# Expert-choice FFN in units of two batches, with half of the add-backs moved into the next attention

## The reference

```python
def _L0_ffn_ref(x, gate_w, w1, w2):            # x: 8 x 512 x 128, E = 8 experts
    probs = softmax(einsum('ntd,ed->nte', x, gate_w))
    g, m = top_k(probs.transpose(0, 2, 1), k)  # k = 128 tokens of each batch for each expert
    xin = x[batch_idx, m]
    h = gelu(einsum('nekd,edf->nekf', xin, w1))          # 128 -> 512
    h = einsum('nekf,efd->nekd', h, w2)                  # 512 -> 128
    return zeros.at[batch_idx, m].add(g[..., None] * h)
...
x = x + ga * _L0_attn_ref(h, ...)
x = x + gb * _L0_ffn_ref(h, ...)               # the rows added back are needed, batch by batch,
x = x + ga * _L1_attn_ref(h, ...)              # before that batch's layer-1 attention
```

## Time and profile before

| | us |
|---|---|
| runs | 1907.9, 1910.45, 1912.4 |
| median | 1910.45 |
| profiled execution | 1909.73 |
| its span | 1907.4 |
| attention 0 and what lies ahead of it | 0 to 814.7 |
| expert-choice FFN | 814.7 to 1013.9 |
| transfers | to 1042.62 |
| attention 1, then the top-2 FFN and the output | to 1907.4 |

### The profile page before, as it was taken

The page is one execution under the profiler, slowest core; times in us unless marked ns, Lnnn a source line. Parts: engine busy times, 40 slices in busy tenths (PEclk is TensorE's granted clock), DMA queues, the critical chain, the costliest instruction groups (busy, mean ns, idle before and its releaser), DMA issues.

```text
span 1907.4 us, 75393 instructions
## 1 busy us (share of the span) xinstructions
PE 1648.4 (86%) x34316; PEld 1268.5 (67%) x34316; DVE 1054.0 (55%) x2219; ACT 695.3 (36%) x1071; POOL 880.8 (46%) x836
## 2 busy tenths in 40 slices
PE   6899999999999988888563889989999998878993
PEld 4567777777777666665342667767777777767883
DVE  3656666666697854536110556665666666544324
ACT  2334444344344323343220333433333433334341
POOL 2555555565646476337886303334242342015442
PEclk9999999999999989999786999999999998989997
DMA  9700000000000000053326223132321313026666
GB/s 305 248 6 2 8 2 7 2 8 2 8 2 8 2 22 20 19 126 35 61 35 117 57 51 81 46 83 51 75 73 44 88 42 84 20 66 183 204 209 183
DMA packets 103847, 128.03 MB, mean 67 GB/s; under 512 B 11909, under 2 KB 86281, under 8 KB 103064
## 3 DMA queue, kind: packets, MB, share of 16 engines
q1 hardware_dynamic: 82920, 103.39, 19.6%
q0 software_dynamic: 15808, 16.93, 4.6%
q10 hardware_dynamic: 4800, 2.89, 0.6%
HBM read 91.57 MB, written 54.07 MB: 76 GB/s over the span
## 4 chain that ended last, share of the span: by engine, by line
PE 59%; DVE 16%; POOL 8%; issue 7%; DMA 5%; ACT 4%; SPq 1%; POOLq 0%; ACTq 0%; DVEq 0%
PE psum L1163 56%; DVE colmax L1853 3%; DMA arena<-in_pack 3%; POOL added_rows L2226 3%; ACT prob L1606 2%; DVE colmax L1963 2%; POOL arena L2214 2%; DVE ctx_sum L1865 2%; DVE raw L1841 1%; DVE rowmax L1860 1%; PE psum L1486 1%; POOL rope_a L2149 1%; POOL rope_b L2151 1%; DVE rowmax L1971 1%; PE psum L1238 1%
## 5 line engine op out<-in xcount | busy, mean ns | idle before, releaser
L1163 PE MATMUL psum<-arena 128*32 128x32 f32 (+8 forms) x10296 | 571.9, 250 | 42.8 <-issue 18.3
L1163 PEld LDWEIGHTS psum<-arena 128*32 128x32 f32 (+3 forms) x10296 | 448.5, 126 | 132.3 <-issue 59.2
L1623 ACT ACTIVATE arena<-psum 128x1024 f32<-128x1024 f32 (+1 forms) x192 | 169.4, 882 | 318.6 <-PE psum L1163 318.6
L1963 DVE TENSOR_REDUCE colmax<-psum 128x256 bf16<-128x768 f32 (+2 forms) x160 | 178.4, 1115 | 88.2 <-PE psum L1163 85.5
L1163 PE MATMUL psum<-prob,ffw 128*32 128x128 f32 x5120 | 204.9, 278 | 23.5 <-DVE rowmax L1860 22.0
L1163 PE MATMUL psum<-neg_ident,rowmax 128*32 128x128 bf16 (+3 forms) x4352 | 210.5, 249 | 4.8 <-issue 3.6
L1853 DVE TENSOR_REDUCE colmax<-psum 128x512 bf16<-128x2048 f32 (+2 forms) x96 | 168.4, 1754 | 77.5 <-PE psum L1163 77.5
L1638 ACT COPY ctx_sum<-psum 128x384 f32<-128x384 f32 x128 | 61.3, 479 | 398.7 <-PE psum L1163 359.1
L2201 POOL TENSOR_TENSOR arena<-ctx_sum 128x256 f32<-128x256 f32 x128 | 94.2, 736 | 221.6 <-DVE ctx_sum L1865 210.0
L1971 DVE TENSOR_REDUCE rowmax<-psum 128x2 bf16<-128x256 f32 (+1 forms) x192 | 98.0, 510 | 137.4 <-PE psum L1163 137.3
L1163 PEld LDWEIGHTS psum<-prob,ffw 128*32 128x32 f32 x5120 | 138.4, 111 | 52.7 <-DVE rowmax L1860 39.4
(11 more groups left out here) (230 smaller groups left out, 2440.0 us busy)
## 6 DMA issues: line engine op xcount, KB each, us to landing
arena<-in_pack SPq DMA_DIRECT2D x39, 578.0 KB, 3.8
sent<-in_empty SPq DMA_DIRECT2D x9, 2112.0 KB, 40.4
arena<-qk_parts SPq DMA_DIRECT2D x96, 128.0 KB
q_copies<-arena SPq DMA_DIRECT2D x32, 256.0 KB, 4.0
prob<-q_copies SPq DMA_DIRECT2D x128, 64.0 KB, 3.3
qk_parts<-arena SPq DMA_DIRECT2D x16, 384.0 KB, 4.2
arena<-sent SPq DMA_DIRECT2D x39, 132.0 KB, 3.2
ffw<-in_L_w SPq DMA_DIRECT2D x16, 256.0 KB, 5.7
```

The lines of the kernel that those rows point to most:

```text
L1163: return pe.matmul(o, lhsT, rhs, start=start, stop=stop, skip_group_check=True)
L1623: act.activation(probs_of(i)[:, :, h0 * P:(h0 + nh) * P], slot(n)[:, 0:(i + 1) * W].rearrange("p (j c) -> p j c", c=W), ACT.Exp, scale=HD1 ...
L1963: dve.tensor_reduce(colmax[:, n % 2, 0:W], slot(n)[:, 0:(i + 1) * W].rearrange("p (j c) -> p c j", c=W), AX.X, ALU.max).then_inc(colmax1_d ...
```

## The change

Groups of `TWO = 2` batches replace groups of four. There are 32 units of 256 columns: group g holds batches 2g and 2g+1, unit r is expert r mod 8 of group r // 8. `hid0`, `xin`, `fetched` and `y_buf` are laid out anew (`y_of`): each group has its own place for `y`, eight slots of two batches.

- Attention 0 carries 20 steps of one gather each, for 16 of two. The other 44 gathers stand in the FFN: 12 ahead of its loop, 32 behind units 12 to 23.
- `rows_in(r + 2)` stands ahead of `down0(r)`, not behind it. `rows_in(0)` and `rows_in(1)` stand ahead of the output projections.
- `send_back` of group 0 stays with its units (0 to 7). That of group 2 stands behind units 24 to 31; those of groups 1 and 3 are single steps in attention 1, one for each of the units 0 to 9, then two for each of the units 10 to 20.
- Only batches 0 and 1 are read back in the FFN (`acc_in`, `x1`). Batch b from 2 on is read at unit 24 (b - 2) + 17 of attention 1 and added at + 21.
- `v_constants` comes in halves; the second waits for group 2's add-backs, since `y` of group 2 lies there.

```diff
+TWO = B // HALF
+UNITS0 = HALF * E
+IN_ATTENTION = 20
...
+        def y_of(r):
+            g, x = divmod(r, E)
+            return y_buf[:, x, :] if g < 2 else fetched[:, 1, x, :] if g == 2 else w1[:, x, 0:TWO * D]
...
-                for k in range(2 * E):
+                for k in range(IN_ATTENTION):
                     late_side.setdefault(n + NU + 10 + k, []).append(
-                        lambda k=k: fetch(k // 2, range(k % 2 * 2, k % 2 * 2 + 2)))
+                        lambda k=k: fetch(k // TWO, range(k % TWO, k % TWO + 1)))
...
+        for k in range(len(choose) // 2):
+            behind.setdefault(3 + k, []).extend(choose[2 * k:2 * k + 2])
+        for k in range(E):
+            behind.setdefault(12 + k // 2, []).append(lambda k=k: fetch(2 * E + k))
+            behind.setdefault(16 + k, []).append(lambda k=k: fetch(3 * E + k))
+            behind.setdefault(3 * E + k, []).append(lambda k=k: send_back(2 * E + k))
+        for r in range(UNITS0):
+            if r + 1 < UNITS0:
                 up0(r + 1)
+            if r + 2 < UNITS0:
+                rows_in(r + 2)
             for f in between.get(r, ()):
                 f()
             add("down0", r=r)
-            if r + 2 < E:
-                rows_in(r + 2)
-            add("send_back", r=r)
+            if r < E:
+                send_back(r)
...
+        n = 0
+        for g in (1, 3):
+            for k in range(E * TWO):
+                behind(n // 2, lambda g=g, k=k: send_back(g * E + k // TWO, range(k % TWO, k % TWO + 1)))
+                n += 1 if n >= 20 else 2
...
-                        if r >= YBUFS:
-                            before = r - YBUFS
-                            for q in range(HALF):
-                                w.wait_ge(d_added[before // E * HALF + q], 16 * (before % E + 1))
+                        if g == 1:
+                            for b in range(TWO):
+                                w.wait_ge(d_added[b], 16 * (x + 1))
```

More of the change, by code:

```diff
@@ L567, in select, with fetch @@
                     [transposed])
-        def fetch(r, batches):
+        def fetch(r, batches=range(TWO)):
             add("fetch", r=r, batches=batches)
@@ L703, in acc_in, with send_back @@
             add("acc_in", b=b)
+        def send_back(r, batches=range(TWO)):
+            add("send_back", r=r, batches=batches)
         def x1(b):
@@ L728, in build @@
         stat_f()
[L729 to L734 removed]
+        for r in range(IN_ATTENTION // TWO, 2 * E):
+            fetch(r)
+        between = {0: [center_f], 2: [router_f], 13: [lambda: x1(0)], 15: [center_a], 17: [lambda: begin(key_a)],
+                   19: [lambda: begin(query_a)], 21: [lambda: x1(1)], 23: [lambda: turn_band(1)]}
+        behind = {1: [norm_f], 9: [lambda: acc_in(0)], 12: [q_cleared], 13: [tokens_a, stat_a],
+                  15: [lambda: add("first_place"), lambda: acc_in(1)],
+                  16: [norm_a], 18: [lambda: qk_parts("key", 0)], 20: [lambda: copies(0)], 21: [lambda: qk_parts("query", 0)],
+                  22: [lambda: turn_band(0)], 25: [lambda: turn_band(2)]}
+        for k in range(len(choose) // 2):
[6 more added lines that the diff above has]
+            if r + 1 < UNITS0:
                 up0(r + 1)
+            if r + 2 < UNITS0:
+                rows_in(r + 2)
             for f in between.get(r, ()):
@@ L738, in build @@
             add("down0", r=r)
[L739 to L741 removed]
+            if r < E:
+                send_back(r)
             for f in behind.get(r, ()):
                 f()
[L744 to L768 removed]
+        q_zero = [s for s in order.steps if s.kind == "q_zero"][0]
         keys_out(0)
@@ L782, in build, with v_ones @@
             stack("query", 0, r)
-        for b in range(HALF, HALF + ABUFS):
-            acc_in(b)
-        add("v_constants", pool=2)
+        v_constants = {}
+        def v_ones(z):
+            v_constants[z] = add("v_constants", pool=1, z=z)
+        v_ones(0)
         def value1(b):
@@ L961, in build @@
         UNITS = B * NU
-        v_constants = [s for s in order.steps if s.kind == "v_constants"][0]
         POOL_KINDS = ("stat", "project", "rotated", "late", "v_constants", "q_zero", "copies", "qk_parts")
@@ L2229, in _ @@
                     elif k == "v_constants":
-                        w.wait_ge(rows_full, 2 * E)
-                        for z in range(2):
-                            chain.wait()
-                            chain.mark(pool.memset(v_head[:, z, :, :].rearrange("p b c -> p (b c)"), 1.0))
+                        z = s["z"]
+                        w.wait_ge(rows_full, UNITS0)
+                        if z:
+                            for b in range(2 * TWO, 3 * TWO):
+                                w.wait_ge(d_added[b], 16 * E)
@@ L2234, in _ @@
+                        chain.wait()
+                        chain.mark(pool.memset(v_head[:, z, :, :].rearrange("p b c -> p (b c)"), 1.0))
                     elif k == "q_zero":
```

145 lines of the change are left out of this document (60 added, 85 removed).

## The result

The kernel after took 1856.11 us at the median (1848.78 to 1858.85), beside a kernel before at 1909.18 us (1903.23 to 1912.40). The ratio is 0.9735, with a 95% interval of 0.9706 to 0.9765. I had forecast 1851. The profiled execution took 1855.61 us, with a span of 1853.8.

What follows compares the result with a forecast made beforehand. POOL's in-order queue of gathers and add-backs was taken to bound the expert-choice FFN, TensorE most of the rest. From 1909.7 us, -11.5 - 3 - 39.4 - 8.9 + 4 = -58.8 gave 1851 us; range 1838 to 1880.

Steps and rivals of the forecast that it cites:

- (a): Attention 0: single gathers shorten nine DVE waits for POOL's rope product by 1.25 us each; -11.5 us, bounds 0 and 18.
- (b): FFN in 32 units of 256 columns: -3 us up to the slots, -39.4 us from there to the last `y` product.
- Slots ready: FFN, choice of slots for batches 4 to 7: ready near 886.5 us for 889.5, -3 us, between 0 and -5.
- The unit read from the layer-1 FFN: New FFN unit taken from the layer-1 FFN: 3.78 us each, two being 7.56 us for 9.32.
- Key and query: FFN behind the slots: PE waits 6.5 us in all for key and query, between 0 and 26.
- (c): Transfers between last `y` product and attention 1: 19.8 us for 28.7, -8.9 us, between 0 and -15.
- The point that the constants come in time: Start of attention 1: POOL's first constants end at 986 to 995 us, DVE needs them about 5 us after 991; just covered.
- (d): 32 add-backs, 59 us of POOL, moved into attention 1's first 21 units: +4 us, between 0 and 30.
- rival 1: Add-backs wait for landings; POOL reaches batch 2's statistics about 15 us late, DVE waits in `center`: 1866 to 1881; chance 0.17.
- It fits by 1.5 us: Attention 1 before batch 2's statistics: 93.6 us of POOL's time, add-backs at 1.85 us each, fit into 95.1.
- rival 4: More than forecast: no stall in the FFN, stack loads in 14 us, attention 0's gain 15 us: 1835; chance 0.06.

Runs made afterwards that it cites:

- e10: Kernel before with only `rows_in(r + 2)` put ahead of `down0(r)` in both loops: 1902.6 us, ratio 0.9983.
- e9: Kernel after with every add-back in the FFN behind its own unit, none in attention 1: 1900.3 us, ratio 1.0001.
- e3: Kernel after with the same 32 add-backs in attention 1 spread one for each of units 0 to 30: 1850.7 us, ratio 0.9713.
- e2: Kernel after without the 32 add-backs in attention 1, that part of the computation left out: 1848.7 us, ratio 0.9671.
- e1: Kernel before with only attention 0's gathers changed, 20 steps of one for 16 of two: 1894.1 us, ratio 0.9920.
- e4: Kernel after with add-backs of groups 2 and 1 mixed, four batches in turn, 24 of these ahead of attention 1: 1850.4 us, ratio 0.9684.
- e5: Kernel after, unchanged, on a second, slower chip: 1951.4 us beside a kernel before at 1979.9, ratio 0.9858.

## Why the prediction was near, and where its steps failed

1. **(a) Attention 0: the term was too small.** Forecast 11.5 us, measured 17.3. The mechanism held: DVE's waits for the rope product fell to 23.9 us, and I had named 27 for 38.6. The step that failed is the one that took DVE's wait for the whole price of the gathers. As a wait it was priced too high: PE's own waits fell by 8.7 us, not 11.3. What was put at nothing is the clock, 9.0 us of slower matmuls, which the earlier trace rows doesn't show. By e10 the same waits can cost 4 us less in clock, so some of the excess over the forecast is chance. The clock column was there to be read, 0.93 in the last 22 units and 1.00 ahead of them. The upper end that I gave, 18 us, held it.
2. **(b) The FFN: right.** Forecast -42.4 us in all, measured -43.7 by the stages. Slots ready: -4.9 from the start of the FFN, for -3. From there to the last `y` product 86.1 us, for 85. The unit read from the layer-1 FFN was the unit that came, 3.74 for 3.78 us. Key and query held PE 5.1 us, for 6.5. Here e9 sharpens what I wrote: without the move of the add-backs the smaller units gain nothing (210.3 us for 206.1). With it they may: two new units take 7.5 us for one of 9.32, which over the ten units of before behind the slots makes some 18 us, an estimate. How that divides from the move wasn't run.
3. **(c) The gap: 6.4 us for 8.9**, 23.0 us where I had 19.8. The five kernels with the same transfers in it on chips of the first kind took 20.2 to 25.0, so the term was just below the lowest of them. The point that the constants come in time was nearly right: DVE waited 2.2 us for them.
4. **(d) The add-backs in attention 1: the forecast failed and rival 1 took place.** Forecast +4, measured +16 in the trace, of which 10.8 in four units. "It fits by 1.5 us" counted 1.85 us for each add-back, with landings that stay at 3.3. They didn't: 6.3 at the median in the gap, 5.7 from 1010 to 1050, and each pair that wasn't covered held everything behind it: POOL came to the statistics 12 us late. The rival named the place (the statistics of batch 2), the engine (DVE in `center`) and 15 us; I gave it 0.17, held back by the share of the DMA engines, 0.25. That was a mean over 82 us. In after the share was 0.65 from 1010 to 1050, where landings took 5.7 us, and 0.36 from 1050 to 1085, where they took 3.3; in before it was 0.42 in the 40 us that match the first of these (1079.5 to 1119.5). What speaks for the cause is e3: the same add-backs, six of them moved behind the statistics, and the stall is gone. By e2 the whole price is 7 to 12 us. (Two sums of the rivals are off, and nothing rests on them: the upper end of rival 1 counts the 4 us of (d) twice, 1877 for 1881, and the three terms of rival 4 come to 1838, not 1835.)
5. **The sum, partly luck.** (a) 5.8 us better and (b) 1.3, (c) 2.5 and (d) 12 worse, and 2.1 from ahead of the change: -53.6 for -58.8 by the spans. The total came close in part since a miss in attention 0 paid for one in attention 1.

The rule of the Trainium skill that I had set beside (d), page "DMA: Bandwidth & Descriptors", section "Issuing engines are not separate DMA queues", has the traces on its side as to landings: 3.3 us at DMA shares of 0.34 and 0.36, 6.3 and up to 10.9 beside the stack loads, 5.7 beside the query loads. The price it would have led to, near 30 us, did not come: late landings held POOL over and over, but POOL's delay reached DVE by more than 2.2 us at one place only, the statistics of batch 2.

## What to carry to other kernels

Where a queue in order mixes work that nobody waits for with work that somebody does, moving the first kind out was worth far more here (e9 against after: 44 us) than a better order of the waiting engine's steps (e10: nothing measurable), and what is moved needs a place with no deadline behind it, not merely a place with idle time. Operations that must wait for their own predecessor to land should be budgeted with a landing measured beside traffic like that of their new place, and that traffic is to be read over the stretch itself, not as a mean over the stage. A wait of TensorE is to be priced with the busy time of the same matmuls at either clock, not by the length of the wait alone.

## What the runs showed of the hardware

- **Short waits also cost clock, by an amount that varies.** The same 1939 matmuls stand in all of these stretches. With 15.1 us of PE's waits for `rowmax`, none over 3.7, both traces of the kernel before had a granted clock of 0.93 and 125.3 us of matmuls; e10, with 15.7 us of the same waits, had 0.96 and 121.0. With 6.4 us of waits, none over 1.8, after and e1 had 1.00 and 116.4 and 116.3 us; e2 and e4 had 0.99 and 118.0.
- **One kernel, two speeds, by the chip or the series.** The kernel before took 1980 us at the median in one series and 1905 to 1909 in the others. Each series of experiments had a chip of its own, so chip and series aren't told apart. The difference isn't in attention 0 (the exponential 22 units ahead of its end starts at 655.1 to 658.1 us on the slow one, at 655.3 to 658.2 elsewhere) but behind it. There PE pauses 1.0 to 1.1 us between few instructions, and ScalarE stands up to 12.6 us at a time for nothing that the trace names (e5). The Trainium skill, page "Runtime: NRT & Kernel Launch", section "Instruction fetch mechanics", says that each engine's sequencer fetches its instructions by a DMA queue of its own, mostly hidden. That these pauses are such fetches isn't shown; the instruction queue moved the same 270 packets on both chips.
- **The spread of one kernel goes mostly with its clock.** e3's executions took 1838.4, 1846.5, 1855.0 and 1861.0 us at mean clocks of 0.975, 0.971, 0.967 and 0.962. Of the 25 of the kernel before on the third chip the fastest (1893.7) had 0.965 and the slowest (1914.8) 0.957. The order isn't always so exact: in after 1856.6 us went with 0.962 and 1858.9 with 0.967.
